# Softmax attention on one core: double gaps with like products together, two buffers for pair results, output normalised in place, inverse sums sent per head

## The chip, the cores and the metric

The kernel runs on one core of one Trainium2 chip. The metric is device time in microseconds (us) of that core, from the start to the end of one execution. Five engines work side by side, each with a queue of its own that runs strictly in order: TensorE (PE, with PEld for its weight loads), VectorE (DVE), ScalarE (ACT), GpSimd (POOL) and SyncE (SP), which here issues the DMAs. They wait for each other by semaphores.

## What is computed

The whole kernel is two transformer layers on x of shape (8, 512, 256): softmax attention, a quantized feed-forward, a decay attention, and a latent attention with sparse experts. The change touches the first part only:

```
q = (x @ Wq).reshape(b, n, 16, 64).transpose(0, 2, 1, 3)
kv = (x @ Wkv).reshape(b, n, 8, 64)
k, v = kv[:, :, :4].transpose(0, 2, 1, 3), kv[:, :, 4:].transpose(0, 2, 1, 3)
q = q * cos + _rotate_half(q) * sin
k = k * cos + _rotate_half(k) * sin
dots = jnp.einsum('bhid,bhjd->bhij', q, repeat(k, 4)) * 64 ** -0.5
attn = jax.nn.softmax(dots, axis=-1)
out = jnp.einsum('bhij,bhjd->bhid', attn, repeat(v, 4)) -> (b, n, 1024)
x1 = _layernorm(x + out @ Wo + bo)
```

## The kernel before

`softmax_attention` (line 679) works on the 8 batches one after the other. A batch is 512 tokens, in four tiles of 128. The engines' queues are not written out step by step but laid out on a table: a round has 64 places ("gaps", `ROUND`, line 735), one for each of the 16 heads x 4 token tiles, and `put(at, engine, keys)` (line 739) hangs steps on a place. A key with a place under 64 belongs to the next batch and runs ahead; one with 64 or more wraps into the following round. Each engine's queue (line 799) is the places in order, and inside a place the order of the `put` calls. A hardware loop runs the queue once per batch (`turns`, line 114), so the round's start is the loop's start.

The steps, with TensorE's first:

- T: x of the next batch is transposed (4 transposes for each of 2 halves). XH, XL on VectorE split it into a high and a low part.
- KV(t), Q(half, t): projections of token tile t, six matmuls of 512 columns each. ROT on VectorE multiplies by the rotary table, VC copies the values out. GpSimd finishes the rotation (Y0, Y1) and splits (HI, LO). VV copies the values on GpSimd.
- KT(g), QT(half, t, b): transposes of keys and queries, four each; C on ScalarE copies them out. KD on SP swaps halves of the keys by DMA.
- S(h, t): scores of head h, tokens of tile t (two matmuls of 512 columns). M on VectorE takes the row maximum, X on ScalarE the exponential with the row sum. Three banks of PSUM hold scores.
- I(h): reciprocal of the row sums on VectorE.
- P(h, c): four transposes of the exponentials. E(h, c) copies them out, even c on VectorE, odd c on ScalarE. Two banks.
- A(p, c): weights times values for pair p, that is heads 2p and 2p+1 (four matmul records). One bank, for all four c.
- RW, RR on SP: the reciprocals of a pair lie one per partition and are needed one per column. RW writes them to DRAM, 4 bytes at a time (line 865), RR reads them back, broadcast to 64 partitions per head, into the one buffer rrep (line 870).
- O(p): VectorE multiplies A's result by rrep into the one buffer ot (line 1058). OH, OL on GpSimd split it into ath and atl (lines 1174, 1178). OH(0) must wait until W(3) of the batch before has read ath (line 1173).
- W(t, part): output projection of token tile t, 12 matmuls of 256 columns for each of two parts; part 1 needs OL(7).
- F, B, G, N on VectorE and EPS, RSTD on GpSimd: the residual is added into r, then the statistics, and r is normalised; ST stores r (two halves of r in turn). XB adds the bias to the residual xb; LB loads it, LX loads xc.

T, KV, Q, KT, QT and W share the two banks of ps_m in turn (line 805); such a product waits for the step that empties its bank (`emptied`, line 806): XL, VC, ROT, C or F. In SP's queue RR(p) stands directly behind RW(p) and waits for its landing (line 868); RW(p) waits for O(p-1) (line 864).

The places around the change: scores of head h at 36 + 4h + c, P and E five later, A of pair p at 36 + 8p + 10, 12, 14 and 15, and O, OH, OL together one after that. So O, OH and OL of pair 0 stand at place 52 of the round, while the W steps of the batch before stand at 48 to 56, with EPS and RSTD two places behind each W.

Of the kernel before, what the change touches and what calls it, by code (L numbers as in the profile page):

```python
# [25 lines left out]
P = 128  # L26
# [652 lines left out]
def softmax_attention(nc, const, x_in, x_out, inverse, w_q, w_kv, w_o, out_bias, rope_tab, name):  # L679
# [6 lines left out]
    with ctx:  # L686
# [33 lines left out]
        stored = [sem(f"stored{s}") for s in range(2)]  # L720
# [14 lines left out]
        ROUND, S0 = 4 * HEADS, 36  # L735
# [10 lines left out]
        attend = lambda p, c: S0 + 8 * p + (10, 12, 14, 15)[c]  # L746
        for g in range(ROUND):
            h, c = g // 4, g % 4
            put(S0 + g + 5, "tensor", ("P", h, c))
            put(S0 + g + 5, "scalar" if c % 2 else "vector", ("E", h, c))  # L750
        for g in range(ROUND):
            h, c = g // 4, g % 4
            put(S0 + g, "tensor", ("S", h, c)); put(S0 + g, "vector", ("M", h, c))
            if c == 3:
                put(S0 + g + 2, "vector", ("I", h))
        for p in range(PAIRS):
            for c in range(TT):
                put(attend(p, c), "tensor", ("A", p, c))
            at = attend(p, TT - 1) + 1
            put(at, "vector", ("O", p)); put(at, "gpsimd", ("OH", p), ("OL", p))  # L760
            put(S0 + 8 * p + 10, "sync", ("RW", p), ("RR", p))

        def project(at, u):
            put(at, "tensor", u)
            put(at + 1, "vector", ("ROT",) + u, *([("VC", u[1])] if u[0] == "KV" else []))
            put(at + 1, "gpsimd", *((n,) + u for n in ("Y0", "Y1", "HI", "LO")))

        def turn_over(at, key):
            put(at, "tensor", key); put(at, "scalar", ("C",) + key)
# [3 lines left out]
        for t, at in enumerate((2, 5, 8, 11)):  # L773
            project(at, ("KV", t))
        for t, (at, back) in enumerate(((14, 18), (17, 22), (21, 26), (25, 29))):
            project(at, ("Q", 0, t))
            for b in range(2):
                turn_over(back + b, ("QT", 0, t, b))
        for g, at in enumerate((16, 20, 28, 40)):
            turn_over(at, ("KT", g)); put(at + 1, "sync", ("KD", g))  # L780
        for t, (at, back) in enumerate(((33, (37, 38)), (39, (43, 44)), (45, (52, 57)), (47, (58, 59)))):
            project(at, ("Q", 1, t))
            for b in range(2):
                turn_over(back[b], ("QT", 1, t, b))
        put(31, "gpsimd", ("VV", 0)); put(46, "gpsimd", ("VV", 1))
        put(63, "gpsimd", ("XB",)); put(63, "sync", ("LB",))
        for t, at in enumerate((48, 50, 53, 55)):
            at += ROUND
            put(at, "tensor", ("W", t, 0)); put(at + 1, "tensor", ("W", t, 1))
            put(at + 2, "vector", ("F", t), ("B", t), ("G", t)); put(at + 2, "gpsimd", ("EPS", t), ("RSTD", t))  # L790
            put(at + 4, "vector", ("N", t)); put(at + 4, "sync", ("ST", t))
        put(ROUND + 2, "sync", ("LX",))
        for g in range(ROUND):
            h, c = g // 4, g % 4
            put(S0 + g, "scalar", ("X", h, c))

        S, ahead, order = {}, {}, {}
        for eng in ENGINES:
# [38 lines left out]
        with nc.Block() as block:  # L837

            @block.sync
            def _(sp):  # L840
                for s in range(2):
                    sp.sem_inc(stored[s], 32)
# [40 lines left out]
                for key in [("LX",)] + [k for k in ahead["sync"] if k[0] != "LB"]:  # L883
                    step(FIRST, -1, key)
# [1593 lines left out]
```

## Time and profile before

| | |
|---|---|
| three runs | 3505.76, 3521.55, 3526.99 us (median 3521.55) |
| the profiled execution, its own time | 3540.68 us |
| its span, first to last instruction | 3538.8 us |
| mean granted TensorE clock | 0.916 |
| PE busy | 2933.0 us, 83% of the span |
| DVE / ACT / POOL busy | 2022.1 / 1333.2 / 963.4 us |
| first attention | from the start to about 1291 us |

Times in the rows are in us from the span's start. A busy PE is not PE at its peak, since the ends of matmuls are modelled. A row of a group gives busy time and mean ns of one instruction; what stands in square brackets or behind "idle" is the engine's idle time before it, and the arrow names what ended it. "issue" is time in which the engine waited for nothing that the profile shows. The granted clock is a share of 2.4 GHz: 1.00 is 2.4 GHz and 0.50 is 1.2 GHz. SPq is SP's queue; a DMA's row shows its issue, not its landing.

### The profile page before, as it was taken

How to read it: one execution, taken by the hardware profiler on the slowest of the kernel's cores; microseconds unless marked ns; L12 is line 12 of the kernel's file. 1: busy time of each engine (PE TensorE's matmuls, PEld its weight loads, DVE VectorE, ACT ScalarE, POOL GpSimd, SP SyncE). 2: the span in 40 equal slices, each digit the busy share in tenths (PEclk: the TensorE clock that was granted, in tenths of full speed). 3: DMA queues.
4: the chain of work that ended last, by engine and by line, in shares of the span. 5: the costliest groups of instructions: out<-in, count | busy, mean ns of one | idle time of the engine just before them, and what ended most of it. 6: DMA issues, size and time to landing. Idle time of an engine off the chain costs nothing. (4 is left out here: it accounts for less than half of the span.)

```text
span 3538.8 us, 61388 instructions
## 1 busy us (share of the span) xinstructions
PE 2933.0 (83%) x16442; PEld 2044.8 (58%) x16443; DVE 2022.1 (57%) x3930; ACT 1333.2 (38%) x2751; POOL 963.4 (27%) x1303
## 2 busy tenths in 40 slices
PE   6999898998989848868999999968888888628883
PEld 4565565655556427756777777734445444327772
DVE  3656565565656547845666666556666666344444
ACT  3545454554545412212222222224444444333332
POOL 3334342332424111123333333210111111122225
PEclk8999999999999979988999999979998898769996
DMA  2111111111111121120000000031222221051115
GB/s 64 31 25 36 33 27 31 31 39 22 37 28 30 25 70 33 44 87 19 12 12 12 12 12 12 7 92 49 59 59 59 59 59 53 17 183 61 59 60 183
DMA packets 190123, 163.18 MB, mean 46 GB/s; under 512 B 85754, under 2 KB 153490, under 8 KB 189330
## 3 DMA queue, kind: packets, MB, share of 16 engines
q1 hardware_dynamic: 178836, 138.40, 14.2%
q0 software_dynamic: 6912, 18.96, 1.4%
q10 hardware_dynamic: 4224, 4.19, 0.3%
q14 instruction: 103, 0.84, 0.3%
q8 instruction: 48, 0.79, 0.1%
HBM read 87.73 MB, written 37.06 MB: 35 GB/s over the span
## 5 line engine op out<-in xcount | busy, mean ns | idle before, releaser
L1120 ACT ACTIVATE soft_probs<-soft_ps_s,soft_mx 128x512 f32<-128x512 f32 x512 | 354.3, 692 | 423.6 <-DVE soft_mx L1042 395.7
L1042 DVE TENSOR_REDUCE soft_mx<-soft_ps_s 128x1 f32<-128x512 f32 x512 | 345.1, 680 | 242.8 <-PE soft_ps_s L952 194.8
L1844 DVE TENSOR_REDUCE mla_mx<-mla_ps_s 128x1 f32<-128x512 f32 x512 | 333.9, 685 | 238.1 <-PE mla_ps_s L1704 207.2
L1947 ACT ACTIVATE mla_pt<-mla_ps_t 128x512 f32<-128x512 f32 x512 | 292.1, 600 | 393.2 <-PE mla_ps_t L1716 358.3
L961 PE MATMUL soft_ps_p<-ident,soft_probs 128*128 128x128 f32 x2048 | 326.9, 284 | 70.6 <-ACT soft_probs L1120 47.7
L952 PE MATMUL soft_ps_s<-soft_ks,soft_qs 128*128 128x512 f32 x1024 | 374.6, 447 | 0.0
L961 PEld LDWEIGHTS soft_ps_p<-ident,soft_probs 128*128 128x128 f32 x2048 | 245.7, 145 | 192.1 <-DVE soft_mx L1042 97.5
L970 PE MATMUL soft_ps_a<-soft_pt,soft_v 128*64 128x512 f32 x1024 | 284.0, 634 | 29.7 <-DVE soft_ri L1046 17.6
L1704 PE MATMUL mla_ps_s<-mla_stack,mla_pad 128*128 128x512 f32 x512 | 233.8, 463 | 23.5 <-DVE mla_mx L1844 18.5
L1052 DVE COPY soft_pt<-soft_ps_p 128x512 f32<-128x512 f32 x256 | 176.1, 688 | 134.3 <-PE soft_ps_p L961 131.3
L1716 PE MATMUL mla_ps_t<-mla_shifted,mla_pad 128*128 128x512 f32 x512 | 223.4, 438 | 28.9 <-ACT mla_pt L1947 26.3
L407 PE MATMUL decay_ps_s<-decay_qs,decay_ks 128*128 128x512 f32 (+3 forms) x1024 | 194.0, 332 | 29.6 <-DVE decay_pt L523 28.7
L523 DVE TENSOR_TENSOR decay_pt<-decay_ps_s,decay_dec 128x512 f32<-128x512 f32 (+3 forms) x512 | 213.7, 481 | 7.2 <-PE decay_ps_s L407 7.2
L407 PEld LDWEIGHTS decay_ps_s<-decay_qs,decay_ks 128*128 128x128 f32 x1024 | 171.7, 197 | 62.3 <-DVE decay_pt L523 41.2
L649 POOL TENSOR_TENSOR decay_rt<-decay_rt 128x256 f32<-128x256 f32 (+1 forms) x192 | 122.6, 660 | 304.8 <-DVE decay_rt L498 304.8
L1704 PEld LDWEIGHTS mla_ps_s<-mla_stack,mla_pad 128*128 128x128 f32 x512 | 103.2, 202 | 165.6 <-DVE mla_mx L1844 80.0
L1148 POOL TENSOR_TENSOR soft_rt<-soft_rt 128x256 f32<-128x256 f32 (+1 forms) x192 | 120.4, 648 | 276.7 <-DVE soft_rt L1029 268.4
L1127 ACT COPY soft_pt<-soft_ps_p 128x512 f32<-128x512 f32 x256 | 148.8, 581 | 67.8 <-PE soft_ps_p L961 30.3
L498 DVE TENSOR_TENSOR decay_rt<-decay_ps_m,decay_rope 128x1024 f32<-128x1024 f32 (+1 forms) x96 | 100.4, 1046 | 125.8 <-POOL decay_st L654 101.2
L313 ACT CAST decay_st<-decay_rt 128x512 fp32r<-128x512 f32 x64 | 39.7, 620 | 332.5 <-POOL decay_rt L649 211.9
L952 PEld LDWEIGHTS soft_ps_s<-soft_ks,soft_qs 128*128 128x128 f32 x1024 | 160.7, 198 | 0.3
L1725 PE MATMUL mla_ps_a<-mla_pt,mla_v 128*32 128x512 f32 x1024 | 151.8, 668 | 8.1 <-ACT mla_pt L1947 5.1
(335 smaller groups left out, 6562.6 us busy)
## 6 DMA issues: line engine op xcount, KB each, us to landing
soft_rrep<-inverse SPq DMA_DIRECT2D x128, 128.0 KB, 3.3
mla_pad<-mla_stack SPq DMA_DIRECT2D x256, 64.0 KB, 2.0
moe_xt<-by_expert SPq DMA_DIRECT2D x72, 129.0 KB
soft_ks<-soft_ks SPq DMA_DIRECT2D x64, 128.0 KB, 2.4
raw<-in_L_ffn_w SPq DMA_DIRECT2D x16, 512.0 KB, 8.4
mla_stack<-mla_yh SPq DMA_DIRECT2D x128, 64.0 KB, 2.1
soft_xc<-in_L_attn_x SPq DMA_DIRECT2D x8, 512.0 KB, 4.7
soft_xb<-in_L_attn_x SPq DMA_DIRECT2D x8, 512.0 KB, 4.0
```

The costliest lines, as they stand in the source:

```text
L407: last = nc.tensor.matmul(ps_s[:, t, P * t:SEQ], ks[:, n, g, P * t:P * t + P], qs[:, h, P * t:SEQ], start=(n == 0), stop=(n == 1))
L523: op = vv.tensor_tensor(weights_of(h, t), ps_s[:, t, P * t:SEQ], dec[:, h, 0:SEQ - P * t], ALU.mult)
L952: last = nc.tensor.matmul(ps_s[:, s_bank(n), :], qs[:, h, P * t:P * t + P], ks[:, b, g, :], start=(b == 0), stop=(b == 1))
L961: last = nc.tensor.transpose(ps_p[:, c % 2, P * t:P * t + P], probs[:, h % 2, t, P * c:P * c + P], ident[:, :])
L970: last = nc.tensor.matmul(ps_a[HD * s:HD * s + HD, 0, :], v[:, 1, c, HD * g:HD * g + HD], weights_of(2 * p + s, c), start=(c == 0), stop=( ...
L1042: op = vv.tensor_reduce(out=mx[:, h, t:t + 1], in_=ps_s[:, s_bank(4 * h + t), :], axis=AX.X, op=ALU.max, negate=True)
L1052: op = vv.tensor_copy(weights_of(h, c), ps_p[:, c % 2, :])
L1120: op = nc.scalar.activation(probs[:, h % 2, t, :], ps_s[:, s_bank(4 * h + t), :], ACT.Exp, bias=mx[:, h, t:t + 1], scale=1.0, accum_out=rs ...
L1704: last = nc.tensor.matmul(ps_s[:, (4 * t + s + 16 * a) % S_BANKS, :], pad[:, QUADS + a, s, P * t:P * t + P], stack[:, a, :], start=True, s ...
L1716: last = nc.tensor.matmul(ps_t[:, s % 2, :], pad[:, a, s, P * t:P * t + P], shifted[:, a, :], start=True, stop=True)
L1844: op = vv.tensor_reduce(out=mx[:, a, t, s:s + 1], in_=ps_s[:, (16 * a + 4 * t + s) % S_BANKS, :], axis=AX.X, op=ALU.max, negate=True)
L1947: op = nc.scalar.activation(pt[:, t % 2, s, :], ps_t[:, s % 2, :], ACT.Exp, scale=KPH ** -0.5)
```

## The change

1. The table works in double gaps: everything on TensorE stands on even places, sorted inside a double gap by kind: P, then T, QT and KT, then A, then S, then projections and W. So a double gap has two P, up to two QT, up to two A, two S, and perhaps one projection. The first scores stand at place 32, P and E six places behind S, A at 12 and 14, O at 18. M and X stand on the odd place behind their S. The projections get new places.
2. ot has two buffers. O(p) waits for OL(p-2) instead of OL(p-1). OH and OL of pair 0 stand at place 60 of the round, those of pair 1 at 62, the others with O.
3. r is gone: F, B, G and N work in xb in place, and the store reads xb. LB waits for all four stores and loads at place 2 of the round in which xb is used.
4. RW and RR run per head, over four rows of DRAM instead of two. In SP's queue they stand as RW(h) at 32 + 4h + 7, RR(h) at 32 + 4h + 10. RR(h) also waits for O of the pair before.
5. S waits for the QT that it needs instead of the last one.

```diff
-        ot = sb("ot", [P, SEQ])
+        ot = sb("ot", [P, 2, SEQ])
-        r = sb("r", [P, 2, D])
-        ROUND, S0 = 4 * HEADS, 36
+        ROUND, S0 = 4 * HEADS, 32
...
+        for h in range(HEADS):
+            for c in range(TT):
+                at = S0 + 4 * h + c // 2 * 2
+                put(at + 6, "tensor", ("P", h, c)); put(at + 6, "scalar" if c % 2 else "vector", ("E", h, c))
+                put(at, "tensor", ("S", h, c)); put(at + 1, "vector", ("M", h, c)); put(at + 1, "scalar", ("X", h, c))
+            put(S0 + 4 * h + 6, "vector", ("I", h))
+            put(S0 + 4 * h + 7, "sync", ("RW", h)); put(S0 + 4 * h + 10, "sync", ("RR", h))
         for p in range(PAIRS):
+            at = S0 + 8 * p
             for c in range(TT):
+                put(at + 12 + c // 2 * 2, "tensor", ("A", p, c))
+            put(at + 18, "vector", ("O", p)); put(at + (28, 22, 18)[min(p, 2)], "gpsimd", ("OH", p), ("OL", p))
+        def project(d, u):
+            put(2 * d, "tensor", u)
+            put(2 * d + 2, "vector", ("ROT",) + u, *([("VC", u[1])] if u[0] == "KV" else []))
+            put(2 * d + 2, "gpsimd", *((n,) + u for n in ("Y0", "Y1", "HI", "LO")))
...
+        for t, d in enumerate((1, 2, 4, 5)):
+            project(d, ("KV", t))
+        for g, d in enumerate((8, 10, 12, 17)):
+            turn_over(d, ("KT", g)); put(2 * d + 1, "sync", ("KD", g))
+        for (half, t), (d, back) in {(0, 0): (6, 9), (0, 1): (8, 11), (0, 2): (9, 13), (0, 3): (12, 15), (1, 0): (13, 16), (1, 1): (16, 19), (1, 2): (17, 20), (1, 3): (21, 24)}.items():
+            project(d, ("Q", half, t))
+            turn_over(back, *turned(("Q", half, t)))
+        put(24, "gpsimd", ("VV", 0)); put(40, "gpsimd", ("VV", 1))
+        put(ROUND + 2, "sync", ("LB",), ("LX",)); put(ROUND + 8, "gpsimd", ("XB",))
+        for t, d in enumerate((24, 25, 28, 29)):
+            at = ROUND + 2 * d
+            put(at, "tensor", ("W", t, 0), ("W", t, 1))
             put(at + 2, "vector", ("F", t), ("B", t), ("G", t)); put(at + 2, "gpsimd", ("EPS", t), ("RSTD", t))
...
+        turn = {"P": 0, "T": 1, "QT": 1, "KT": 1, "A": 2, "S": 3, "Q": 4, "KV": 4, "W": 4}
+        for d in range(0, ROUND, 2):
+            gaps[d, "tensor"] = sorted(gaps.get((d, "tensor"), []) + gaps.pop((d + 1, "tensor"), []), key=lambda k: turn[k[0]])
...
                     elif kind == "RW":
-                        j, p = own(i, key), key[1]
-                        hold(sp, *dve_s.at(j, "I", 2 * p + 1))
-                        hold(sp, *(dve_s.at(j, "O", p - 1) if p else dve_s.at(shift(j, -1), "O", PAIRS - 1)))
-                        sp.dma_start(inverse.rearrange("s (t p) -> p s t", p=P), ri[:, 2 * p:2 * p + 2, :], allow_slow_non_contiguous=True).then_inc(inverse_out, 16)
+                        j, h = own(i, key), key[1]
+                        hold(sp, *dve_s.at(j, "I", h))
+                        hold(sp, *(dve_s.at(j, "O", h // 2 - 2) if h >= 4 else dve_s.at(shift(j, -1), "O", PAIRS + h // 2 - 2)))
+                        sp.dma_start(inverse[h % 4].rearrange("(t p) -> p t", p=P), ri[:, h, :], allow_slow_non_contiguous=True).then_inc(inverse_out, 16)
...
+                        hold(sp, *(dve_s.at(j, "O", h // 2 - 1) if h >= 2 else dve_s.at(shift(j, -1), "O", PAIRS - 1)))
+                        sp.dma_start(rrep[HD * (h % 2):HD * (h % 2) + HD, :], inverse[h % 4].partition_broadcast(HD)).then_inc(inverse_in, 16)
...
-                            dve.wait_ge(*(pool_s.at(j, "OL", p - 1) if p else pool_s.at(shift(j, -1), "OL", PAIRS - 1)))
-                            op = vv.tensor_tensor(ot[:, :], ps_a[:, 0, :], rrep[:, :], ALU.mult)
+                            dve.wait_ge(*(pool_s.at(j, "OL", p - 2) if p >= 2 else pool_s.at(shift(j, -1), "OL", PAIRS + p - 2)))
+                            op = vv.tensor_tensor(ot[:, p % 2, :], ps_a[:, 0, :], rrep[:, :], ALU.mult)
...
-                            op = vv.tensor_tensor(r[:, t % 2, :], ps_m[:, bank["W", t], 0:D], xb[:, t, :], ALU.add)
+                            op = vv.tensor_tensor(xb[:, t, :], ps_m[:, bank["W", t], 0:D], xb[:, t, :], ALU.add)
```

## Rows read from the trace of the kernel before

**Rows 1.** Busy time by stretch: start:end, length, busy us (x instructions) by engine, PEclk, DMA, GB/s.

```profile
115.57:1031.28 915.71, 835.11 (x4610) 539.86 (x4609) 529.53 (x935) 448.76 (x1080) 333.64 (x449) 0.96 0.14 31
...
555.70:562.50 6.80, 5.67 (x20) 3.81 (x20) 5.24 (x13) 3.77 (x9) 1.58 (x4) 0.50 0.12 40
...
1181.00:1291.00 110.00, 82.78 (x435) 50.76 (x434) 49.03 (x92) 40.08 (x100) 17.85 (x22) 0.89 0.10 24
```

**Rows 2.** Who waited for whom, 100 to 1200 us: us in total, times, longest.

```profile
POOL soft_ath L1174 <- PE soft_ps_m L979: 120.1, 7, 17.3
...
PE soft_ps_a L970 <- DVE soft_pt L1052: 12.0, 13, 2.0
```

**Rows 3.** Timeline, the W steps of one round: start, us, engine, line, tiles, [idle before].

```profile
539.82 0.39 PE L979 MATMUL soft_ps_m<-soft_woh,soft_ath 128*128 128x256 f32 x1 [0.79 <-DVE soft_r L1066]
...
551.09 0.61 POOL L1174 CAST soft_ath<-soft_ot 128x512 fp32r<-128x512 f32 x1 [17.28 <-PE soft_ps_m L979]
...
554.27 0.41 DVE L1078 TENSOR_SCALAR soft_r<-soft_r,soft_mv,soft_rstd 128x256 f32<-128x256 f32 x1 [11.14 <-POOL soft_rstd L1187]
...
556.83 1.11 PE L961 MATMUL soft_ps_p<-ident,soft_probs 128*128 128x128 f32 x4 [5.91 <-ACT soft_probs L1120]
```

**Rows 4.** SP's own waits, 100 to 1300 us, and its timeline behind the last round.

```profile
SPq L42 <- DMA inverse<-soft_ri: 574.8, 60, 11.2
...
1242.95 0.37 SPq L865 DMA_DIRECT2D inverse<-soft_ri  x1
1253.11 1.09 SPq L870 DMA_DIRECT2D soft_rrep<-inverse  x2
1258.08 0.37 SPq L865 DMA_DIRECT2D inverse<-soft_ri  x1
```

**Rows 5.** DMA issues, 100 to 1200 us: KB each, median us to landing.

```profile
x<-soft_r SPq DMA_DIRECT2D x28, 128.0 KB, 1.7
soft_xb<-in_L_attn_x SPq DMA_DIRECT2D x7, 512.0 KB, 4.0
```

**Rows 6.** Timeline of TensorE: single A steps in a round, three together at the end.

```profile
618.31 0.71 PE L952 MATMUL soft_ps_s<-soft_ks,soft_qs 128*128 128x512 f32 x2
618.95 1.08 PE L970 MATMUL soft_ps_a<-soft_pt,soft_v 128*64 128x512 f32 x4
619.96 0.66 PE L935 MATMUL soft_ps_m<-ident,soft_st 128*128 128x128 f32 x4
620.45 0.60 PE L961 MATMUL soft_ps_p<-ident,soft_probs 128*128 128x128 f32 x4
620.81 0.71 PE L952 MATMUL soft_ps_s<-soft_ks,soft_qs 128*128 128x512 f32 x2
...
621.36 0.38 PE L940 MATMUL soft_ps_m<-ident,soft_kst 128*128 128x128 f32 x2
...
1261.78 3.03 PE L970 MATMUL soft_ps_a<-soft_pt,soft_v 128*64 128x512 f32 x12
1264.74 0.39 PE L979 MATMUL soft_ps_m<-soft_woh,soft_ath 128*128 128x256 f32 x1
```

**Rows 7.** Timeline at the start of a round, TensorE and VectorE.

```profile
418.14 0.60 PE L961 MATMUL soft_ps_p<-ident,soft_probs 128*128 128x128 f32 x4
...
421.43 0.71 PE L952 MATMUL soft_ps_s<-soft_ks,soft_qs 128*128 128x512 f32 x2
...
426.15 0.69 DVE L1042 TENSOR_REDUCE soft_mx<-soft_ps_s 128x1 f32<-128x512 f32 x1 [6.99 <-issue]
...
426.35 1.11 PE L961 MATMUL soft_ps_p<-ident,soft_probs 128*128 128x128 f32 x4 [4.21 <-ACT soft_pt L1127]
...
429.40 0.68 DVE L1052 COPY soft_pt<-soft_ps_p 128x512 f32<-128x512 f32 x1
```

**Rows 8.** Groups of instructions, 100 to 1100 us: busy us, mean ns, idle before.

```profile
L1029 DVE TENSOR_TENSOR soft_rt<-soft_ps_m,soft_rope 128x1024 f32<-128x1024 f32 (+1 forms) x80 | 82.3, 1029 | 7.0 <-POOL soft_st L1159 7.0
```

**Rows 9.** Timeline of TensorE, the last output products.

```profile
1274.89 0.55 PE L979 MATMUL soft_ps_m<-soft_woh,soft_ath 128*128 128x256 f32 x1 [8.45 <-POOL soft_atl L1178]
```

More of the change, by code:

```diff
@@ L719, in softmax_attention @@
         inverse_out, inverse_in, swapped = sem("inverse_out"), sem("inverse_in"), [sem(f"swapped{g}") for g in range(KVH)]
-        stored = [sem(f"stored{s}") for s in range(2)]
+        stored = sem("stored")
         hold = gated_hold(const["held"])
@@ L756, in softmax_attention @@
         for p in range(PAIRS):
+            at = S0 + 8 * p
             for c in range(TT):
[L758 to L766, printed above, removed]
@@ L771, in softmax_attention, with turn_over @@
+        def turn_over(d, *keys):
+            for key in keys:
+                put(2 * d, "tensor", key); put(2 * d, "scalar", ("C",) + key)
         for k in range(KD):
             put(0, "tensor", ("T", k)); put(0, "vector", ("XH", k), ("XL", k))
[L773 to L789, printed above, removed]
+        for t, d in enumerate((1, 2, 4, 5)):
+            project(d, ("KV", t))
@@ L840, in _ @@
             def _(sp):
-                for s in range(2):
-                    sp.sem_inc(stored[s], 32)
+                sp.sem_inc(stored, 16 * TT)
                 (raw_q, _, _), (raw_kv, _, _), (raw_o, _, _) = raw_and_parts
@@ L881, in _ @@
                 sp.dma_start(bias[:, :], out_bias.partition_broadcast(P)).then_inc(bias_in, 16)
-                sp.dma_start(xb[:, :, :], batch(x_in, 0)).then_inc(xb_loaded, 16)
-                for key in [("LX",)] + [k for k in ahead["sync"] if k[0] != "LB"]:
+                for key in [("LX",)] + ahead["sync"]:
                     step(FIRST, -1, key)
@@ L893, in _ @@
                         step((BATCH - 1, 0), BATCH - 1, key)
-                for s in range(2):
-                    hold(sp, stored[s], 32 * BATCH + 32)
+                hold(sp, stored, 16 * TT * (BATCH + 1))
             @block.tensor
@@ L1173, in steps @@
                                 hold(pool, *pe_s.at(shift(j, -1), "W", TT - 1, 1))
-                            op = nc.gpsimd.tensor_copy(ath[:, p, :], ot[:, :])
+                            op = nc.gpsimd.tensor_copy(ath[:, p, :], ot[:, p % 2, :])
                         elif kind == "OL":
@@ L2406, in build @@
         counts = ctx.enter_context(nc.sbuf_tensor("counts", [P, E_], F32))
-        inverse = nc.dram_tensor("inverse", [2, SEQ], F32, kind="Internal").ap()
+        inverse = nc.dram_tensor("inverse", [4, SEQ], F32, kind="Internal").ap()
         softmax_attention(nc, const, a["L0_attn_x"], x1, inverse, a["L0_attn_Wq"], a["L0_attn_Wkv"], a["L0_attn_Wo"], a["L0_attn_bo"], a["rope0"], "soft")
```

39 lines of the change are left out of this document (10 added, 29 removed).

## The prediction

> **What bounds the kernel now.** I read the table of stretches first. The change touches only the first attention, which ends at 1291 us; everything behind it keeps its time. From the first group of transposes of batch 1 (115.57 us) to that of batch 7 (1031.28 us) lie six rounds in 915.71 us, 152.6 us each, and TensorE is busy for 91% of them [rows 1]. The last attention steps, behind the last round, take another 110 us with TensorE at 75%. So TensorE is the bound inside the rounds, but not a full one.
>
> What interrupts it stands in the list of waits: seven waits of GpSimd for the output product, 120.1 us in all [rows 2]. The timeline of one round links them [rows 3]. OH of pair 0 stands in GpSimd's queue ahead of RSTD of tile 1, and it waits for W(3), the last reader of the old ath: 17.28 us. RSTD(1) is behind it, so N(1) on VectorE waits 11.14 us; the E and M steps behind N(1) are late, ScalarE's exponentials too, and TensorE stands still for 5.91 us. The kernel does this to itself once per round, by an order alone.
>
> The second limit is SP. It sends 1/sum through DRAM, and of the span's first 1300 us it spent 574.8 us in 60 waits for the small write: 9.6 us each [rows 4]. In the last steps nothing covers that: write issued at 1242.95, read issued at 1253.11, the next write at 1258.08. One pair of heads takes 15.1 us there, set by this chain and not by TensorE.
>
> **Part 1: OH and OL of the first pairs moved behind W, with two ot buffers.** In the new table OH(0) has place 60 of the round and W(3) place 58, so GpSimd reaches RSTD of tiles 0 to 2 without waiting. ot has two halves, so O(1) (place 58) needs no OL(0). Gone: 5.91 us; the 0.79 us of the output product's wait for F (it now has the other misc bank and a gap more) [rows 3]; and what the idle stretch did to the clock. In the 6.80 us from 555.70 on the granted clock is 0.50, that is 1.2 GHz, behind that idle stretch [rows 1]; 5.67 us of it are work, which at 2.4 GHz takes 2.9, so 2.7 us are lost. Seven times 9.4 us: **-66 us**. What is late next: N(t) still waits for RSTD(t), one double gap behind G(t), but GpSimd has nothing ahead of EPS and RSTD any more, and a double gap lasts some 4 us (about 130 us of work in 32 of them); if something stood there again, the 5.91 us would come back. r goes away: F, B and N work in xb, same shapes, same price; the store reads xb, and LB waits for all four stores (1.7 us each to land [rows 5]) at place 2. XB comes three double gaps later, while the load lands in 4.0 us [rows 5]: hidden. If that cover went, GpSimd's queue would stand up to some 4 us.
>
> **Part 2: like products together.** Two A steps now stand side by side. A single one starts 0.64 us after the scores before it (618.31 to 618.95) where another product starts after 0.55 us (620.81 to 621.36), and takes 1.01 us; three in a row take 2.96 us, 0.99 each [rows 6]. Joined, a pair saves 0.09 + 0.04 = 0.13 us; 16 pairs in each of 8 batches: **-17 us**. The order P to A and A to S is shown nowhere; an entry could cost up to 0.14 us more, which takes the whole saving, or 0.1 less. Bounds: 0 and -30 us. P beside P and S beside S save nothing I can see. A also comes one double gap behind the E it needs; in the rounds of before TensorE waited 12.0 us in all for such an E [rows 2], behind O, ROT and VC in VectorE's queue: **-12 us**.
>
> **Part 3: new waits of the double gap.** ps_m has two banks. Walking through the new order, the second QT of (0,0) at double gap 9 has the bank of Q(0,1), a product of the gap before, which ROT empties; so has the second QT of (0,2) at 13, with Q(0,3). In VectorE's queue ROT stands behind E(c even), I and O of that gap, and E waits for the P that opens the gap. From the gap's start: four transposes 0.66 us from their first start to their last end [rows 6], then E and O at 0.65 us each (five operations in a row took 3.25 us, 426.15 to 429.40 [rows 7]), ROT 1.03 us [rows 8] and the small I: 3.05 us. P and S together take 0.91 us (620.45 to 621.36 [rows 6]), half of it each, and QT has the shape of P, so TensorE is ready after 1.35 us. It waits 1.7 us, with A or S queued behind. Q(1,2) at gap 17 waits for ROT of Q(1,1) in the same way, from 2.25 us on: 0.8 us. In seven rounds 7 x (2 x 1.7 + 0.8) = **+30 us** (in batch 0 GpSimd is the limit anyway). Bounds: 0, if VectorE were early, and 45.
>
> At the round's start VectorE now does E, XH, XL, XH, XL before the two M; before, M came first. M, XH, XL, XH, XL took the same 3.25 us [rows 7]; now M comes about 2.5 us later, and the scores of the next gap need its exponentials: I take 1.5 us. In five of seven rounds the start is also where ScalarE and VectorE stand still with nothing to wait for (6.99 us, "issue") while TensorE runs ahead and then waits 4.21 us [rows 7]. It can run ahead by 2.7 us of work now (two P, both T, two S) and did 3.8 before (from 418.14 to the end of the scores that began at 421.43, 0.55 us later): 1.1 us more. 5 x 2.6 + 2 x 1.5 = **+16 us**; bounds 0 and 30.
>
> **Part 4: inverse sums per head.** RW now writes 512 numbers instead of 1024, and RR reads one row. SP's queue is strictly RW(h), RR(h), RW(h+1): each RR waits for its own write to land, so one head costs the landing L plus 0.7 us for issues and holds, and two heads must fit in what a pair takes, about 18 us in the rounds. L of 512 numbers is not in the trace. From below: a 128 KB store lands in 1.7 us [rows 5]. From above: 9.6 us, the landing of 1024 [rows 4]. I take the middle, 5.65 us, since the packets are the same 4 bytes and half as many, and a big store with few packets is fast: what costs must be the number. Then SP needs 2 x (5.65 + 0.7) = 12.7 us per pair, hidden in the rounds. Behind the last round TensorE needs 8 x 0.9 + 4 x 1.03 = 11.3 us per pair, so SP sets 12.7 instead of 15.1: 5 x 2.4 = 12 us. The last output product, which waited 8.45 us for OL(7) [rows 9], waits about 4 us less: **-16 us** together. Bounds: -25 to +28 (5 x 5.6, if L stays 9.6), and in that case the rounds grow, below.
>
> The Trainium skill speaks against this part. "DMA: Bandwidth & Descriptors", section "Anatomy of one DMA", has a transfer cost about 2.0 us fixed plus its bytes, most of it the receipt of the last write, heaviest for HBM. The trace disagrees in size: 4 KB took 9.6 us [rows 4], the rule gives 2.0. If the rule holds in kind (a fixed receipt, here large), halving the numbers halves nothing, and that is the rival that ends slower. The same page's "Specifications" says that pieces under 512 B are read, modified and written, which would go with their number and gives what I chose.
>
> **Sum.** -66 - 17 - 12 + 30 + 16 - 16 = -65 us. The profiled execution took 3540.7 us (span 3538.8), so 3476 us, a factor of 0.982. The median of the runs shown is 3521.55, 0.5% lower; the same factor gives **3457 us**.
>
> **The rivals.**
> (a) *The small write does not get shorter* (slower). L stays near 9.6 us: SP needs 2 x 10.3 = 20.6 us per pair, 165 us per round and about 6 more for its own standstill at the loop's start, 171 instead of 152.6: 7 x 18 = +129, and +28 behind the rounds. 3698, or 3678 on the scale of the median. It decides from L of about 8 us on, where two heads no longer fit in 18 us. For it: the sixteen counts of a write come late, as if of a receipt. Against: the packets that other stores need are larger and fewer, and land in 1.7 us. 0.14.
> (b) *VectorE's queue gives it back* (within 1%). The joining of A saves nothing (+17), the new waits take their upper bounds (+15, +14): 3522, or about 3503. For it: VectorE's order inside a gap is fixed, and E at its head waits for the newest product. Against: between the new places all buffers are free a gap ahead. 0.18.
> (c) *TensorE becomes the bound without gaps* (faster still). Only the first parts and the end count, the new waits hide behind A: -66 - 30 - 12 - 25 = -133: 3408, or 3389. 0.06.
> My forecast has 0.62; its own range is 3420 to 3500.
>
> One per cent is 35 us, about what a measurement of this kernel can tell from no change; the line for faster lies at 3486. Of the forecast's 0.62 I put 0.58 below it, with (c) and a little of (b) 0.68. Same: 0.17. Slower: (a) and its half-way cases, 0.15. Range 3405 to 3545: it leaves (a) and most of (c) out.
>
> **What would show each step.** Right: no wait of GpSimd for the output product, none of VectorE for rstd over 2 us; rounds of 143 to 146 us; SP's waits for the small write at 5 to 6 us each, 128 of them; a TensorE wait for ROT of 1 to 2 us twice per round at the second QT. Wrong: SP's waits still above 8 us, with VectorE's O waiting for rrep in every pair; or rounds of about 150 us with the GpSimd wait gone, which would mean that a wait I have not seen took its place.

## The result and the profile after

The changed kernel takes 3674.7 us (3662.4 to 3683.6, four runs) beside 3518.9 for the kernel before: ratio 1.044 [1.040, 1.049], slower. I had forecast 3457, so the sign is wrong. Rival (a), the small write that does not get shorter, is what happened; it had named 3678.

The table of stretches, six rounds and then the steps behind the last round, in the columns of [rows 1]:

```profile
127.63:1133.79 1006.16, 827.56 (x4611) 580.84 (x4610) 529.18 (x937) 437.39 (x1084) 336.08 (x450) 0.92 0.18 30
1301.50:1428.00 126.50, 73.34 (x360) 45.48 (x360) 39.69 (x77) 29.84 (x77) 16.76 (x21) 0.78 0.14 20
```

A round takes 1006.16 / 6 = 167.7 us instead of 152.6. TensorE's work is no larger (827.56 us busy, before 835.11) and VectorE's is the same; TensorE is busy for 82% of a round instead of 91%. The second stretch is 126.5 us instead of 110.0, but the two do not start at the same place of the table: counted from the P steps of place 64, the first behind the last round (1183.02 before, 1296.33 here), it is 131.7 instead of 108.0. So the time is waiting. SP's own waits, 100 to 1400 us:

```profile
SPq L42 <- DMA inverse<-soft_ri: 992.6, 124, 10.8
SPq L42 <- ACT soft_ks L1097: 41.2, 10, 6.6
SPq L42 <- DVE soft_ri L1033: 3.5, 3, 1.7
SPq L42 <- DVE soft_ot L1045: 0.4, 1, 0.4
```

The first row answers to [rows 4]: 992.6 us in 124 waits, 8.0 us each, where 574.8 us in 60 stood before. The last two show that SP almost never waits for VectorE's sums or for O: it never catches up with the work, it is what the others wait for. From issue to the last of its sixteen counts a write of 512 numbers takes 9.2 us (median, from the semaphore records of the trace). Where that time goes is seen in the records of the DMA packets: of the write issued at 669.82 every 4-byte packet lies between 0.9 and 1.7 us behind the issue, and its counts come from 5.7 to 8.5 us behind it. The DMA engines are soon done with their packets; what is long is the time from there to the counts. How that reaches TensorE, from the list of waits inside the six rounds (127 to 1134 us):

```profile
POOL soft_ath L1159 <- DVE soft_ot L1045: 335.6, 36, 17.8
...
PE soft_ps_a L957 <- DVE soft_ot L1045: 70.3, 18, 12.6
...
PE soft_ps_m L922 <- DVE soft_rt L1016: 59.3, 12, 12.7
```

The row of [rows 2] in which GpSimd waited for the output product is gone from this list, as Part 1 said. In its place TensorE waits for O (the one bank of A) and, in the second QT, for ROT. The timeline shows that this second wait is the first one again, handed on. SP, then VectorE, then TensorE in one round:

```profile
669.82 0.38 SPq L854 DMA_DIRECT2D inverse<-soft_ri  x1
678.43 0.45 SPq L859 DMA_DIRECT2D soft_rrep<-inverse  x1
679.13 0.38 SPq L854 DMA_DIRECT2D inverse<-soft_ri  x1
...
688.62 0.46 SPq L859 DMA_DIRECT2D soft_rrep<-inverse  x1
```

```profile
685.46 0.69 DVE L1045 TENSOR_TENSOR soft_ot<-soft_ps_a,soft_rrep 128x512 f32<-128x512 f32 x1 [4.99 <-DMA soft_rrep<-inverse]
686.07 1.21 DVE L1016 TENSOR_TENSOR soft_rt<-soft_ps_m,soft_rope 128x1024 f32<-128x1024 f32 x1
```

```profile
687.34 1.11 PE L922 MATMUL soft_ps_m<-ident,soft_st 128*128 128x128 f32 x4 [6.80 <-DVE soft_rt L1016]
```

Write issued at 669.82, its read at 678.43, the next write at 679.13: 9.3 us for one head. O has waited for the read (fifteen of its sixteen counts are there by 681.3, the last at 685.3, with the next small write under way), ROT stands behind O, and the second QT stands still for 6.80 us until ROT has emptied its bank. A list of waits names ROT there; the timeline names the transfer. Sixteen heads at 9.3 to 10 us make 150 to 160 us of a round of 167.7.

Behind the last round the chain is bare, as in [rows 4], but with one head per link:

```profile
1388.16 0.45 SPq L859 DMA_DIRECT2D soft_rrep<-inverse  x1
1388.79 0.45 SPq L854 DMA_DIRECT2D inverse<-soft_ri  x1
1397.88 0.45 SPq L859 DMA_DIRECT2D soft_rrep<-inverse  x1
1398.51 0.45 SPq L854 DMA_DIRECT2D inverse<-soft_ri  x1
```

That is 9.7 us per head and 19.4 per pair, where a pair took 15.1. The last output product, TensorE's row that answers to [rows 9], waits longer instead of 4 us less:

```profile
1412.88 0.55 PE L966 MATMUL soft_ps_m<-soft_woh,soft_ath 128*128 128x256 f32 x1 [10.31 <-POOL soft_atl L1163]
```

### The profile page after: what moved, and what is told of

Same layout as the page of the kernel before. It is cut to its first block and busy times, and to the rows that moved or that the text cites. A ratio compares the mean times of both kernels' runs of the same rounds, so it can differ in the third digit from the quotient of the medians.

```text
span 3680.3 us, 61969 instructions
## 1 busy us (share of the span) xinstructions
PE 2939.6 (80%) x16442; PEld 2103.0 (57%) x16443; DVE 2019.9 (55%) x3930; ACT 1317.5 (36%) x2751; POOL 963.4 (26%) x1303
## 5 line engine op out<-in xcount | busy, mean ns | idle before, releaser
L1029 DVE TENSOR_REDUCE soft_mx<-soft_ps_s 128x1 f32<-128x512 f32 x512 | 330.5, 685 | 206.5 <-PE soft_ps_s L939 193.3
L957 PE MATMUL soft_ps_a<-soft_pt,soft_v 128*64 128x512 f32 x1024 | 273.0, 658 | 129.4 <-DVE soft_ot L1045 81.2
L939 PE MATMUL soft_ps_s<-soft_ks,soft_qs 128*128 128x512 f32 x1024 | 329.1, 442 | 10.6 <-ACT soft_probs L1105 10.5
L948 PE MATMUL soft_ps_p<-ident,soft_probs 128*128 128x128 f32 x2048 | 275.8, 279 | 39.2 <-issue 20.9
L939 PEld LDWEIGHTS soft_ps_s<-soft_ks,soft_qs 128*128 128x128 f32 x1024 | 181.2, 201 | 159.6 <-issue 55.4
L957 PEld LDWEIGHTS soft_ps_a<-soft_pt,soft_v 128*64 128x64 f32 x1024 | 67.0, 145 | 235.9 <-issue 135.3
L1045 DVE TENSOR_TENSOR soft_ot<-soft_ps_a,soft_rrep 128x512 f32<-128x512 f32 x64 | 43.6, 682 | 252.5 <-DMA soft_rrep<-inverse 186.3
L1159 POOL CAST soft_ath<-soft_ot 128x512 fp32r<-128x512 f32 x64 | 39.1, 610 | 512.4 <-DVE soft_ot L1045 512.4
```

The source lines that it names most:

```text
L939: last = nc.tensor.matmul(ps_s[:, s_bank(n), :], qs[:, h, P * t:P * t + P], ks[:, b, g, :], start=(b == 0), stop=(b == 1))
L948: last = nc.tensor.transpose(ps_p[:, c % 2, P * t:P * t + P], probs[:, h % 2, t, P * c:P * c + P], ident[:, :])
L957: last = nc.tensor.matmul(ps_a[HD * s:HD * s + HD, 0, :], v[:, 1, c, HD * g:HD * g + HD], weights_of(2 * p + s, c), start=(c == 0), stop=( ...
L1029: op = vv.tensor_reduce(out=mx[:, h, t:t + 1], in_=ps_s[:, s_bank(4 * h + t), :], axis=AX.X, op=ALU.max, negate=True)
```

## The experiments

Twelve kernels in three sets; each set ran on one chip with the kernel before beside it. Before took 3536, 3506 and 3475 us in the three, so ratios are compared across sets and times only within one.

**1. The changed kernel with the transfer per pair.**

```diff
-            put(S0 + 4 * h + 7, "sync", ("RW", h)); put(S0 + 4 * h + 10, "sync", ("RR", h))
+            put(at + 11, "sync", ("RW", p), ("RR", p))
```

RW and RR themselves are those of the kernel before.

> The changed kernel with the transfer of inverse sums per pair again, as before (one write of 1024 numbers, both reads behind it, at place 11 of the pair); all else as changed. Theory F (the write takes some 9 us to land whether it carries 512 or 1024 numbers, so per head SP needs about 2 x 9.9 us per pair and becomes the bound): with one write per pair the rounds fall from 167 us to about 145, the time to 0.98 of the kernel before, about 3460. Theory G (the double gaps themselves make it slower, the transfer hardly matters): it stays above 1.02 of the kernel before.

3454.96 us beside 3536.03: ratio 0.976 [0.973, 0.978]. Its stretches and SP's wait:

```profile
120.83:973.17 852.34, 793.31 (x4610) 566.45 (x4609) 534.00 (x938) 439.11 (x1084) 337.17 (x450) 0.99 0.16 35
1115.20:1208.00 92.80, 67.44 (x356) 43.62 (x352) 37.13 (x74) 28.77 (x75) 15.44 (x20) 0.87 0.11 24
```

```profile
SPq L42 <- DMA inverse<-soft_ri: 477.3, 49, 11.3
```

Rounds of 142.1 us. The per-head transfer alone turns 0.976 into 1.044, a factor of 1.070, and everything else in the change gains 2.4%. This run also holds the waits of Part 3, undisturbed:

```profile
259.98 1.09 PE L948 MATMUL soft_ps_p<-ident,soft_probs 128*128 128x128 f32 x8 [3.49 <-issue]
...
266.06 0.73 PE L939 MATMUL soft_ps_s<-soft_ks,soft_qs 128*128 128x512 f32 x2 [1.85 <-ACT soft_probs L1105]
```

```profile
319.43 0.66 PE L922 MATMUL soft_ps_m<-ident,soft_st 128*128 128x128 f32 x4 [1.70 <-DVE soft_rt L1016]
```

and from its list of waits in the six rounds:

```profile
PE soft_ps_m L922 <- DVE soft_rt L1016: 23.3, 12, 3.0
PE soft_ps_p L948 <- issue: 22.0, 6, 4.0
...
PE soft_ps_s L939 <- ACT soft_probs L1105: 7.6, 6, 1.9
...
PE soft_ps_m L110 <- DVE soft_rt L1016: 4.6, 6, 0.8
```

**2. The kernel before with the transfer per head alone.**

```diff
-            put(S0 + 8 * p + 10, "sync", ("RW", p), ("RR", p))
+                put(S0 + 4 * h + 6, "sync", ("RW", h)); put(S0 + 4 * h + 9, "sync", ("RR", h))
```

> The kernel before with the transfer per head and nothing else changed. Theory F: SP needs 2 x (9.2 + 0.7) = 19.8 us per pair, where a round of 152.6 us gives 19.1 on average, plus SP's own standstill at the loop's start; rounds of about 165 us and 4.7 us more per pair behind the last round: 1.03 of the kernel before, about 3630. Theory G: within 1% of the kernel before.

3789.46 us, ratio 1.073 [1.070, 1.075]; rounds of 178 to 188 us, where I had expected 1.03 and 165 us. The sign was right and the size less than half: from 503.88 on SP needs 10.3, 10.2, 12.4, 11.5 and 9.8 us from one write to the next, where I had reckoned 9.9. But it is the same factor as between 1 and the changed kernel (1.070), from the other side: the edit costs 7% in either table.

**3. Two writes in flight.** RR(h) behind RW(h+1) in SP's queue, with a semaphore for even and one for odd heads.

```diff
-            put(S0 + 4 * h + 7, "sync", ("RW", h)); put(S0 + 4 * h + 10, "sync", ("RR", h))
+            put(S0 + 4 * h + 7, "sync", ("RW", h)); put(S0 + 4 * h + 12, "sync", ("RR", h))
```

> The changed kernel, with RR(h) placed behind RW(h+1) in SP's queue and a semaphore for even and one for odd heads, so that two writes of 512 numbers are under way at a time. Theory F with a landing that is mere latency: two landings overlap, SP needs about 11 us per pair, 0.98 of the kernel before, about 3455. If the landings hold each other up (one after the other at a shared place), each takes up to 18 us and the time stays near that of the changed kernel, 1.04.

3566.68 us, ratio 1.007 [1.005, 1.010]; rounds of 156 to 161 us. SP's waits:

```profile
SPq L42 <- DVE soft_ri L1033: 506.1, 93, 12.0
SPq L42 <- ACT soft_ks L1097: 110.1, 22, 8.1
SPq L42 <- DMA inverse<-soft_ri: 102.5, 56, 5.4
```

The landings overlap (each still takes about 9 us, but SP's waits for them fall from 992.6 to 102.5 us). A little over half of the loss is back. The rest looks like order again: the read of a pair's second head now stands behind the write of the next pair's first head, which waits for sums that do not exist yet (506.1 us in the first row). Two writes under way at once hardly lengthen each other (8.9 us by median), so it was the chain of SP's queue and not what the DMA engines can carry.

**4. The numbers 64 B apart.** The read takes a fixed row of the input, so the normalisation by the sums is left out.

```diff
-inverse[h % 4].rearrange("(t p) -> p t", p=P)
+inverse[h % 4].rearrange("(t p x) -> p t x", p=P, x=16)[:, :, 0]
...
-inverse[h % 4].partition_broadcast(HD)
+x_in[0, 0:2, :].rearrange("a d -> (a d)").partition_broadcast(HD)
```

> The changed kernel, with the 512 numbers of a write laid down 64 bytes apart instead of 4; RR reads a fixed row of the input instead of the sums, so the output is not normalised by them, with all waits kept. If the landing is long because neighbouring 4-byte writes meet in the same 64 bytes and are done one after the other, it falls from 9.2 us to under 5 and SP's waits with it, time about 3460 to 3480. If it is a cost per piece or a plain receipt, it stays at 9 us and the time near 3675.

One run, 3418.3 us; rounds of 138 to 141 us. SP's wait, and the row of the DMA issues (KB, median us to landing):

```profile
SPq L42 <- DMA inverse<-soft_ri: 166.3, 89, 5.3
```

```profile
inverse<-soft_ri SPq DMA_DIRECT2D x124, 2.0 KB, 2.3
```

The same 512 pieces of 4 B land in 2.3 us instead of 9.2, and the whole loss is gone. So neither the number of pieces nor the receipt of a write costs 9 us; that the numbers lie side by side does. Both answers between which Part 4 chose, a cost per number and a fixed receipt, fall with it.

**5. Pieces of 16 B.** Each partition's four numbers side by side; O reads the row in the matching order.

```diff
-inverse[h % 4].rearrange("(t p) -> p t", p=P)
+inverse[h % 4].rearrange("(p t) -> p t", p=P)
...
-op = vv.tensor_tensor(ot[:, p % 2, :], ps_a[:, 0, :], rrep[:, :], ALU.mult)
+op = vv.tensor_tensor(ot[:, p % 2, :].rearrange("q (t p) -> q t p", t=TT), ps_a[:, 0, :].rearrange("q (t p) -> q t p", t=TT), rrep[:, :].rearrange("q (p t) -> q t p", t=TT), ALU.mult)
```

> The changed kernel with one thing different: the row in DRAM is laid out token-in-tile first, so each partition's four numbers lie side by side and the small write has 128 pieces of 16 B instead of 512 of 4 B; the multiplication reads the row in the matching order. Theory (writes that meet in the same 64 B follow one another): 4 partitions share 64 B instead of 16, so the landing is 2.3 + 6.9 x 3/15 = 3.7 us instead of 9.2, two heads need under 9 us of SP, rounds of 138 to 142 us, 3420 to 3445 us. Rival 1 (any sharing of 64 B costs the full landing, or a fixed receipt): landing about 9 us, 3675 us. Rival 2 (the strided reading makes VectorE's multiplication slow): landing short, but O above 1 us and rounds of 143 or more, 3450 to 3480 us.

3401.87 us beside 3506.47: ratio 0.969 [0.967, 0.971], with all of the computation in it.

```profile
114.28:971.82 857.54, 796.37 (x4610) 565.92 (x4609) 550.01 (x937) 438.57 (x1084) 336.55 (x450) 0.98 0.14 35
```

```profile
SPq L42 <- DVE soft_ot L1045: 340.5, 62, 10.4
SPq L42 <- DMA inverse<-soft_ri: 161.9, 90, 5.2
```

The landing is 2.3 us, shorter than the 3.7 that I had drawn by a straight line. SP now waits for O instead of O for SP. O itself takes 1.04 us instead of 0.68 with its strided operand, and the wait of the second QT behind it grew from 1.70 to 2.08 us (so the timeline rows of kernels 1 and 5; the 1.87 and 2.24 in the expectations stand in no row), so rival 2 is right in kind, and its 143 us per round came true though its 3450 us did not: the rounds take 142.9 us, the one that reads in order (4) about 140. That is no less than the 142.1 us of kernel 1. What kernel 5 gains on kernel 1 lies behind the last round: 76.5 us from place 64 on (1113.97 to 1190.5), where kernel 1 needs 98.8 (1109.16 to 1208.0).

**6. ROT one place earlier**, in kernel 1.

```diff
-            put(2 * d + 2, "vector", ("ROT",) + u, *([("VC", u[1])] if u[0] == "KV" else []))
+            put(2 * d + 1, "vector", ("ROT",) + u, *([("VC", u[1])] if u[0] == "KV" else []))
```

> The changed kernel with the transfer per pair again (3455 us) and ROT and VC one place earlier, so that VectorE empties the bank of a projection ahead of the next double gap's E. Theory (Part 3: the second QT waits for ROT because it stands behind E and O): the waits of 1.87 us twice and 0.93 us once per round go, 7 x 4.7 = 33 us, 3422 to 3435 us. Rival (VectorE's queue gives it back): the 1.0 us of ROT now stands ahead of E and M, so P or S waits instead; within 10 us of 3455 or slower, up to 3480 us.

3473.40 us, ratio 0.991 [0.989, 0.992], where kernel 1 has 0.976: slower by 1.5%. VectorE, then TensorE, in one round:

```profile
316.88 1.23 DVE L1016 TENSOR_TENSOR soft_rt<-soft_ps_m,soft_rope 128x1024 f32<-128x1024 f32 x1 [4.83 <-POOL soft_st L1144]
```

```profile
318.75 1.97 PE L948 MATMUL soft_ps_p<-ident,soft_probs 128*128 128x128 f32 x8 [1.86 <-DVE soft_pt L1039]
```

The rival is right. ROT writes the one buffer rt, which GpSimd still reads: VectorE stands still for 4.83 us with E behind it, and now P waits, 24 times in six rounds, up to 3.00 us. The 1.70 us of Part 3 are real, but they are not to be had by moving ROT alone.

**7. OH and OL of pair 0 moved, in the kernel before.**

```diff
-            put(at, "vector", ("O", p)); put(at, "gpsimd", ("OH", p), ("OL", p))
+            put(at, "vector", ("O", p)); put(at if p else 57, "gpsimd", ("OH", p), ("OL", p))
```

> The kernel before with OH and OL of pair 0 alone at place 57 of the round instead of 52, behind the last output product; nothing else. Theory (Part 1): GpSimd's 17 us wait ahead of RSTD goes, 9.4 us per round, 7 times, 66 us: ratio 0.981, about 3470 us beside 3536. Rival (the wait is only handed on: with one ot buffer O(1) waits for OL(0), and W has what is left of it): ratio 0.992 to 1.0, 3508 us or more.

3475.84 us, ratio 0.992 [0.990, 0.994]: 31 us, not 66. GpSimd's wait is down to 1.8 us per round and the 5.91 us behind it are gone, but half of it came back at another place. SP, then VectorE, then TensorE:

```profile
547.28 1.10 SPq L870 DMA_DIRECT2D soft_rrep<-inverse  x2
548.72 1.07 SPq L874 DMA_DIRECT2D x<-soft_r  x2
```

```profile
551.25 0.42 DVE L1066 TENSOR_TENSOR soft_r<-soft_ps_m,soft_xb 128x256 f32<-128x256 f32 x1 [3.57 <-DMA x<-soft_r]
```

```profile
551.81 1.01 PE L935 MATMUL soft_ps_m<-ident,soft_st 128*128 128x128 f32 x4 [3.28 <-DVE soft_r L1066]
```

The row at 551.25 is F(3). It writes the half of r that the store of tile 1 still reads, and a QT waits for the bank that F empties. That store comes late, though N(1) ended at 537.8: it stands in SP's queue behind a small write issued at 535.93, whose landing holds SP until 547.2; then the stores of tiles 1 and 2 go out together (548.72), the first lands at 551.2, and F(3) starts. This is so in every round (six waits, 20.1 us). So not the rival that I had written down (OL of pair 0), but the same slow write once more, by way of a store. In the change r is gone and F writes xb, where no store stands before it, so this wait can't arise; I had booked that edit at nothing. No run has the other parts of the change with r still there, and none has kernel 7 with a faster write, so what r's going is worth by itself is not shown.

**8. The kernel before with pieces of 16 B**, nothing else (the same two lines as in 5, for a pair).

> The kernel before with the rows in DRAM laid out token-in-tile first, 256 pieces of 16 B instead of 1024 of 4 B per pair; nothing else. Theory: landing 3.7 us instead of 9.6. In the rounds of this kernel that was hidden, so only the steps behind the last round gain: five pairs from 15.1 to about 11.3 us and less of the last wait, together 20 to 25 us: ratio 0.993 to 0.995. Rival (the landing stays): no difference, ratio 0.998 to 1.002. Rival 2 (the landing was not hidden in the rounds either, O waited for it): 40 us or more, ratio under 0.989.

3446.62 us, ratio 0.983 [0.979, 0.986]: 60 us, more than the 20 to 25 of the theory, from that one layout. That is the range of rival 2, and its sign is there as well: in the six rounds of the kernel before O waited 20.1 us in 15 waits for the read of the sums, in this one not once. But TensorE's list has no wait for O in either, so that this is where the time came from is not shown. Its stretches, and VectorE's standstill without a releaser inside the rounds:

```profile
113.78:1007.52 893.74, 823.86 (x4610) 533.94 (x4609) 547.27 (x935) 448.77 (x1080) 334.38 (x449) 0.98 0.13 32
1156.50:1238.00 81.50, 70.93 (x410) 43.16 (x408) 47.98 (x87) 36.30 (x92) 16.81 (x21) 1.00 0.10 28
```

```profile
DVE soft_mx L1042 <- issue: 2.3, 1, 2.3
```

From place 64 on it needs 84.2 us (1153.78 to 1238.0) instead of 108.0, and 3.7 us less per round. The second part I did not expect; it is taken up in the last section.

**9. The numbers 8 B apart** (normalisation left out, as in 4), eight to 64 B.

```diff
-inverse[h % 4].rearrange("(t p) -> p t", p=P)
+inverse[h % 4].rearrange("(t p x) -> p t x", p=P, x=2)[:, :, 0]
```

> The changed kernel with the 512 numbers 8 B apart in DRAM instead of side by side; the read takes a fixed row of the input, so the normalisation by the sums is left out. Eight numbers share 64 B, in place of 16 (landing 9.2 us) or one (2.3 us). Theory A (the landing grows with the number of 4-byte writes in the same 64 B): 2.3 + 6.9 x 7/15 = 5.5 us, and SP then needs 12.4 us per pair, rounds of 140 to 142 us, about 3415 us. Theory B (two of the transfer's sixteen parts meeting in one 64 B are what costs; if a part is eight partitions, eight numbers 8 B apart fill just one 64 B): landing 2.3 us, about 3415 us too. So only the landing tells them apart. Theory C (only numbers directly side by side collide, whoever writes them): 2.3 us as well, and the shifted run below separates it from B.

```profile
inverse<-soft_ri SPq DMA_DIRECT2D x123, 2.0 KB, 4.1
```

4.1 us: between 2.3 (alone in 64 B) and 9.2 (sixteen in 64 B). Theory C, which says 2.3, falls, and so does B if a part is eight partitions, as I had assumed; A stays in kind, though the growth is not a straight line (it would give 5.5). The time, one run of 3377.9 us beside 3474.6, shows that 4.1 us are hidden as well (0.972; kernel 4 has 0.967).

**10. Pieces of 16 B, every row moved by 32 B.**

```diff
-inverse[h % 4].rearrange("(p t) -> p t", p=P)
+inverse[h % 4, 8:8 + SEQ].rearrange("(p t) -> p t", p=P)
```

> The kernel with 16 B pieces (landing 2.3 us, 3402 us) with every row moved by 32 B from a multiple of 64 B, so that the seam between groups of eight partitions falls inside a 64 B stretch; four pieces share 64 B as before. Theory A (number of writes per 64 B) and theory C (4-byte neighbours): landing stays at 2.3 us, 3402 us. Theory B (parts of one transfer meeting in one 64 B): landing rises to between 3 and 9 us, and above 8 us the time goes back to about 3670.

```profile
inverse<-soft_ri SPq DMA_DIRECT2D x124, 2.0 KB, 2.2
```

2.2 us and 3392.7 us (one run): where the rows begin does not matter. With parts of eight partitions or of four, the shift lets two parts meet in a 64 B stretch, so B falls here whichever it is.

**11 and 12. O behind ROT in VectorE's queue, and XH, XL behind the two M as well**, both in kernel 5.

```diff
-            put(at + 18, "vector", ("O", p)); put(at + (28, 22, 18)[min(p, 2)], "gpsimd", ("OH", p), ("OL", p))
+            put(at + (28, 22, 18)[min(p, 2)], "gpsimd", ("OH", p), ("OL", p))
...
             turn_over(back, *turned(("Q", half, t)))
+        for p in range(PAIRS):
+            put(S0 + 8 * p + 18, "vector", ("O", p))
```

```diff
-            put(0, "tensor", ("T", k)); put(0, "vector", ("XH", k), ("XL", k))
+            put(0, "tensor", ("T", k)); put(1, "vector", ("XH", k), ("XL", k))
```

> The kernel with 16 B pieces (3402 us beside 3506) with one order changed: in VectorE's queue O stands behind the ROT of its gap instead of ahead. Theory: the second QT waits for ROT behind E and O, 2.24 us twice per round, and Q(1,2) 1.33 us; O took 1.04 us of each. Taking O out of the way gives back 3 x 1.04 x 7 = 22 us: 3380 us, ratio 0.963; the waits become 1.2 and 0.3 us. Rival (as when ROT went a place earlier: O is late, so A or P waits in turn): within 5 us of 3402 or slower.

> As the one with O behind ROT, and XH and XL of the next batch one place later, behind the two M of the round's first gap. Theory: M is no longer 2.6 us late at the round's start, so TensorE's wait for the next scores (1.8 to 2.65 us in pieces_16) goes, 7 x 2 = 14 us: 3366 us, ratio 0.959. Rival: the E of the next gap is behind XL now and the first KV waits for XL's bank, the same time in another place: within 5 us of the run with O behind ROT.

3383.23 us, ratio 0.972 [0.969, 0.975], and 3379.71 us, ratio 0.972 [0.969, 0.975]. By the ratios neither differs from kernel 5 (0.969 [0.967, 0.971]), which ran in another set; in this set kernel 10, which has kernel 5's table, took 3392.7 in its single run, with rounds of 143.0 us beside 141.0 and 139.6 here. TensorE's waits for ROT in the rounds are down from 24.9 us in 12 (kernel 5) to

```profile
PE soft_ps_m L924 <- DVE soft_rt L1018: 18.0, 24, 1.1
...
PE soft_ps_m L110 <- DVE soft_xtl L1008: 9.1, 6, 1.6
```

in kernel 12: each is about a third as long (0.75 us beside 2.1) and there are twice as many, and the wait for scores at the round's start has become one for XL's bank, as the rival of 12 said. The rounds did get shorter by 2.0 and 3.4 us beside kernel 10, but the time by 9.5 and 13 us beside its single run, where I expected 22 and 36. Kernels 5, 11 and 12 all beat both the kernel before and the changed one; an order among them is not shown.

## Why the prediction was wrong

**The step that failed** is one number in Part 4: "I take the middle, 5.65 us", between 1.7 and 9.6, "since the packets are the same 4 bytes and half as many". It measured 9.2 us. The landing of 512 adjacent numbers is that of 1024, so halving the numbers took off 0.9 us (10.1 to 9.2) and not half. With 5.65 a head costs 6.4 us of SP and two fit beside the 18 us of a pair; with 9.2 they cost 19 to 20. The term changed from -16 to +220 (3680.3 - 3459.6, the spans of the changed kernel and of kernel 1; by the ratios 1.044 and 0.976 about 240), since on the far side of 18 us every microsecond counts sixteen times in each round. I had written the threshold down myself (8 us) and saw that 9.6 lay beyond it. The ends were far apart, and the nearest row, the same write of twice the size, said 9.6. I argued instead from a store with larger packets. The chance of 0.14 for rival (a) had no better basis than that. The reason given for the middle, that the number of pieces is what costs, fell with kernel 4: the same 512 pieces, 64 B apart, land in 2.3 us.

**Rival (a) in numbers.** It gave rounds of 171 us; they took 167.7. It gave 28 us behind the rounds; from place 64 on it was 23.7 (131.7 - 108.0). It ended at 3678 on the scale of the median: 3674.7.

**Part 1** (-66): GpSimd's wait went and the 5.91 us with it, but the move alone gave 31 us in the kernel before (kernel 7), because SP's queue held the store that F(3) needs; the forecast had no such wait, and in the change it can't arise. The price of the clock was probably too low: TensorE's busy time fell from 835.11 to 793.31 us over six rounds at a granted clock of 0.96 and 0.99, 7.0 us per round, of which joining A explains 2.6. That leaves 4.4, where I had 2.7; that all of it is clock is only argued.

**Part 2** (-17 and -12): in the changed kernel at 810 us,

```profile
809.03 1.03 PE L948 MATMUL soft_ps_p<-ident,soft_probs 128*128 128x128 f32 x8
810.00 1.94 PE L957 MATMUL soft_ps_a<-soft_pt,soft_v 128*64 128x512 f32 x8
811.86 1.19 PE L939 MATMUL soft_ps_s<-soft_ks,soft_qs 128*128 128x512 f32 x4
812.89 1.04 PE L948 MATMUL soft_ps_p<-ident,soft_probs 128*128 128x128 f32 x8
813.68 1.23 PE L939 MATMUL soft_ps_s<-soft_ks,soft_qs 128*128 128x512 f32 x4
```

From P to S with two A between takes 2.83 us, without 0.79: 2.04 for the two. A single one cost 1.65 - 0.55 = 1.10 [rows 6], so a pair saves 0.16 where I had 0.13; 128 of them, 20 us. Right. The waits of A for an E are gone (not in kernel 1's list). Right.

**Part 3** (+30 and +16): the second QT waits 1.70 us in kernel 1's row and 1.94 on average (23.3 us in twelve waits), I had 1.7; Q(1,2) waits 4.6 us in six rounds, 0.77 each, my 0.8. The scores of the round's start wait 1.85 us in the row above, 1.3 on average (7.6 us in six); I had 1.5. P's wait at the loop's start came to 22.0 us in six rounds; in the kernel before TensorE's waits there came to 18.1 (3.33, 4.21 as in [rows 7], 4.37, 4.06 and 2.15, once none). Both together grew by 11.5 us in six rounds, 13 in seven. So +30 and +16 were both about right.

**What no part had.** Without Part 4 my sum was -49 us; the spans say 3459.6 - 3538.8 = -79. So Parts 1 to 3 together were too careful by 30 us, and Part 4 was off by 236. Behind the last round kernel 1 needs 98.8 us from place 64 on instead of 108.0, with the old transfer: the first scores stand at place 32 instead of 36, so less is left (392 matmul records by the tables instead of 424; the stretches shown start at other places, so their 356 and 435 can't be compared). The first batch pays over half of that back (120.83 instead of 115.57 us). So most of the 30 us lies in the rounds. In six of them TensorE's busy time fell by 41.8 us, where my parts make 29 (2.7 for the clock and 2.1 for A in each), and its idle time by 21.6 (80.6 to 59.0), where they make 12.

**The page that I set against Part 4.** "DMA: Bandwidth & Descriptors" of the Trainium skill, section "Anatomy of one DMA", has a transfer cost about 2.0 us fixed plus its bytes. The section measured that for DMAs that GpSimd issues, which the prediction left out; here SP issues them. For the writes that do not crowd one another the trace agrees: 2.3 us for 2 KB (kernels 4, 5 and 10) and for 4 KB (kernel 8). For adjacent 4-byte writes it does not: 9.2 us. What follows from a fixed cost, that halving a small transfer gains almost nothing, was right, and I gave it too little weight.

## What to carry to other kernels

When a queue issues a write, waits for it and then issues its read, the number of such round trips is the cost, not the bytes: before splitting one transfer into two, write down (trips per round) x (landing) against the round, and take the landing from the nearest measured transfer. Where values that lie one per partition must go through DRAM, lay each partition's values side by side, even if the reader must then stride: that one edit was worth 1.7% in the kernel before and 7% in the changed one. And an edit that removes a wait needs the buffer behind it too: ask which store or engine still reads what the freed step writes, and what stands ahead of that store in its queue.

## What the runs showed of the hardware

**Small writes that crowd a short stretch of DRAM are slow.** Median from issue to the last count, 512 numbers unless said:

| layout in DRAM | writes per 64 B | us |
|---|---|---|
| 4 B, 64 B apart (kernel 4) | 1 | 2.27 |
| 16 B pieces, 128 of them (5), moved by 32 B (10) | 4 | 2.29, 2.23 |
| 16 B pieces, 256 of them (8) | 4 | 2.29 |
| 4 B, 8 B apart (9) | 8 | 4.12 |
| 4 B, adjacent (changed kernel; 2) | 16 | 9.2; 9.5 |
| 4 B, adjacent, 1024 of them (before; 1) | 16 | 10.1; 10.2 |

Some counts of the last two rows are missing from the trace (in 10 of 128 writes of the changed kernel, 22 of 64 of before); the last count that is there was taken. That such writes are carried out one behind another in the same short stretch fits all rows but is only argued. Nor is 64 B shown as its length: any from 16 B up to a whole row of 2 KB orders these layouts in the same way, since only the number of writes per byte differs. What 4-byte pieces four to 64 B would do, no run tells. Twice the numbers in the same layout take only 1 us more, so it is how densely the writes lie and not the sum of them that sets the time.

**They also hold up the start of the loop.** In [rows 7] VectorE stood still for 6.99 us with nothing to wait for. In the six rounds of the kernel before such standstills came to

```profile
ACT soft_pt L1127 <- issue: 22.1, 4, 5.9
DVE soft_mx L1042 <- issue: 15.2, 3, 7.0
```

and in kernel 8, whose code differs only in the layout (of the write, and of how O reads), to 2.3 us for VectorE (row above), 3.1 for TensorE and none for that step of ScalarE. Kernels 4, 10, 11 and 12 have none at all in their rounds, kernel 5 has 8.2 us, kernel 9 (landing 4.1 us) 10.7 on ScalarE; kernel 1 has 22.0 us on TensorE.

The records of the DMA packets have one kind that fits: packets of 8 KB that bring instructions. At the loop's start of [rows 7] two of them, at 419.47 and 420.19, took 3.28 and 3.21 us with no other packet under way, while the small write issued at 415.92 had no count yet (they came from 424.7 to 426.1, and VectorE went on at 426.15). Over the six rounds such a packet took 2.2 us (median of 60) in the kernel before and 0.38 (of 60) in kernel 8. So the slow writes hold up other transfers that begin while they are under way. That the engines stood still for these very instructions is likely but not shown: VectorE went on 3.4 us after the first of the packets had ended.

This is a share of what the layout is worth to a kernel in which I had called the transfer hidden, and not most of it. By the two traces 24 us of it lie behind the last round and 22 in the six rounds. Of the 22, TensorE's waits at the loop's start make 11 (18.1 to 7.1), and its busy time another 11, at a granted clock of 0.96 and 0.98.
